# A one-layer language-model tower on one core: idle-time products on TensorE, weight pieces and rank reads regrouped

## The chip, the core and the metric

The kernel runs on one core of a Trainium2 chip. The metric is the time of one execution on the device in microseconds (us), the median of several runs. The five engines of the core are TensorE (PE; its weight loads are shown apart as PEld), VectorE (DVE), ScalarE (ACT), GpSimd (POOL) and SyncE (SP), which only issues transfers here. Engines run their own instruction lists in order and wait for each other through semaphores.

## The reference, cut to what matters

```python
h = tok(x)                                  # softmax of 4 coefficients per token times 4 base rows, + bias; 4096 tokens x 256
p = layernorm(h) @ Wv.T + bv                # q = k = v = p, 16 heads of 16, batches of 1024 tokens
attn = softmax(p_h @ p_h.T / 4) @ p_h       # per head, 4 batches
h = h + attn @ Wo.T + bo
logits = layernorm(h) @ router              # 8 experts, the 2 best of each token, softmax of the two
hidden = silu(xn @ w13_gate) * (xn @ w13_up)   # 512 wide, per expert
h = h + sum over the two experts of weight * (hidden @ w2)
```

## The kernel before

Everything runs in one launch. `attention` comes first, then `experts`. Attention works in 16 groups (`GROUPS`), four per batch of 1024 tokens (`HG` is 4); a group is four heads. Of each group there are 64 score tiles of 128x512 (items). Three items make a unit: PE computes them (`scores`, L347), ACT takes their exponential in one 128x1536 instruction (L758), and PE sums four of them at a time against the values (`sums`, L359). PE's program is written out by hand: behind each such quad the function `after` may place other products, by the quad's number in its group: `fold` and `turn` of the group before, `tile_rows`, the two halves of the next group's query features (`query_product`, L334), and `rank`.

In some groups PE prepares the next batch: `preparing(grp, 1)` is true in groups 1, 5 and 9 (tokens are turned, L479), `preparing(grp, 2)` in groups 2, 6 and 10 (keys are turned, L485); in group 12 `worst_own` (L530) stands at the same place. Each of these three waits for `u_read` of the second half, that is for DVE's instruction L788 of that half.

DVE has one list per group: the normalisation of the group before last, `fold_out`, `places_out`, `copy_rows`, then `query_features` half 0 (L786, L788, L790, L794), `choose` (the two best experts, L829 to L837), `query_features` half 1, `weigh` (L898 to L900), `rank_read_out` (L905 to L907), and at the end the copy of the accumulated sums out of PSUM (L1245), on which `fold` waits. In the last group (`LAST`, 15) it also does, before that copy, what is left of group 14: `rank_read_out`, `places_out` (to L923), `normalise` (L842 to L859) and `normal_rows` (L868 to L871).

POOL works beside this on the expert weights. Each of 24 pieces (512 KB) is loaded by SP (L256), and split into a bf16 high part (a cast, L700) and a bf16 low part (a subtraction of two SBUF operands, L631). `pieces_of` deals the first 19 (`BESIDE`) out to the groups, one each and two in groups 5, 10 and 15. Between them POOL writes the slots of the tokens (`note`, L637). Of the last five pieces ACT makes the high part once the exponentials are over (L732), POOL the low one; a load may start once the low part three pieces back is done.

The tail of attention is a chain between DVE and PE: copy of the sums (L1245), `fold` (L379), `turn` (L386), `last_rows` (L414), `choose`, `rank` (L435), the tile counts and places on DVE, `slot_table` (L419, L421), and the indices (L962) by which POOL gathers the rows of the first four expert tiles. SP turns them by DMA; PE's first expert product (L1472) and DVE's L1549 wait for the first of them. PE meanwhile does a last product on `near_p` (L624) and twelve products without use (L626), and then walks the expert tiles.

Set-up does the same for the constants and the first batch: `weights_and_keys`, `turn_tokens`, `turn_keys`, `own_scores`, then the two query products of group 0.

## Time and profile before

| | us |
|---|---|
| median of 3 runs | 871.98 |
| lowest and highest | 871.75, 874.14 |
| the profiled execution | 876.0 |
| its span, first to last instruction | 874.2 |
| PE busy in the span | 767.1 |
| ACT busy | 544.6 |
| DVE busy | 510.9 |
| POOL busy | 355.0 |

The profiled execution took 876.0 us, of which 1.8 us lie outside the span. Times in the rows below are counted from the start of the span. Attention with its tail ends at about 579 us, the experts take the rest. A row of the timeline gives the start, the duration, the engine, the line of the kernel, the operation and its operands, how many instructions were merged, and in brackets how long the engine had been idle before and what ended that.

### The profile page before, as it was taken

What the parts mean: (1) busy time and instruction counts of PE and PEld (TensorE: products, weight loads), DVE (VectorE), ACT (ScalarE), POOL (GpSimd) and SP (SyncE); (2) the same over time, 40 slices, a digit from 0 to 9 for tenths busy, and PEclk for the clock granted to TensorE, in tenths of its full rate; (3) what the DMA queues carried; (4) which work ended last, traced back from release to release, by engine and by line L of the source; (5) the groups of instructions that cost most, each with busy time, mean ns of one, the idle gap of its engine ahead of it and who ended that gap; (6) DMA issues with size and microseconds to landing.
All of it is one profiled execution on the core that took longest, in us unless ns stands there. A gap on an engine that the chain in (4) does not pass through costs nothing.

```text
span 874.2 us, 16623 instructions
## 1 busy us (share of the span) xinstructions
PE 767.1 (88%) x5249; PEld 300.0 (34%) x5250; DVE 510.9 (58%) x1623; ACT 544.6 (62%) x515; POOL 355.0 (41%) x305
## 2 busy tenths in 40 slices
PE   3699994999999999989999997289999999999992
PEld 1233220222222222222222221135555555555551
DVE  7644563576667558676756478654555555545540
ACT  0468993999989999989999997312222222222221
POOL 6760030302411330241133217256666666666652
PEclk9589996899999999999999999579999999999997
DMA  2030105012011101201110124349999999999973
GB/s 40 2 94 1 37 12 38 13 37 74 13 37 49 46 16 37 74 14 37 49 50 14 37 73 98 87 85 166 159 162 164 158 162 163 160 163 156 154 122 44
DMA packets 141362, 67.72 MB, mean 77 GB/s; under 512 B 114822, under 2 KB 136984, under 8 KB 141294
## 3 DMA queue, kind: packets, MB, share of 16 engines
q1 hardware_dynamic: 125262, 49.33, 27.5%
q0 software_dynamic: 16032, 17.55, 13.9%
q8 instruction: 35, 0.57, 0.4%
q14 instruction: 33, 0.27, 0.2%
HBM read 22.52 MB, written 17.57 MB: 46 GB/s over the span
## 4 chain that ended last, share of the span: by engine, by line
PE 69%; DVE 16%; ACT 5%; issue 5%; DMA 2%; another core or an unknown queue 1%; POOL 0%; SPq 0%; POOLq 0%; ACTq 0%; DVEq 0%
PE PS L359 20%; PE PS L1472 18%; PE PS L1481 10%; PE PS L347 9%; ACT shared L758 5%; PE PS L402 2%; PE PS L379 2%; DVE room L788 2%; DVE room L794 2%; PE PS L403 2%; DVE room L786 2%; PE PS L445 1%; DMA room<-room 1%; DVE room L790 1%
## 5 line engine op out<-in xcount | busy, mean ns | idle before, releaser
L758 ACT ACTIVATE shared<-PS 128x1536 f32<-128x1536 f32 x342 | 464.8, 1519 | 48.5 <-PE PS L347 36.3
L359 PE MATMUL PS<-shared,va 128*32 128x512 f32 x2048 | 279.8, 619 | 5.1 <-DVE room L1245 4.7
L637 POOL DMA_INDIRECT slots<-pair_no,room x60 | 59.5, 991 | 364.3 <-DVE room L917 350.6
L1472 PE MATMUL PS<-w_p,room 128*128 x816 | 186.7, 379 | 0.0
L347 PE MATMUL PS<-room,ak 32*128 32x512 bf16 x1024 | 137.5, 394 | 14.3 <-ACT shared L758 9.5
L1522 ACT ACTIVATE shared<-PS 128x512 f32<-128x512 f32 x68 | 40.6, 598 | 162.9 <-PE PS L1472 162.9
L1438 POOL DMA_INDIRECT out<-room,idx_tok x68 | 110.9, 1631 | 67.1 <-ACT room L1527 38.6
L1553 DVE SCALAR_TENSOR_TENSOR shared<-shared,room,PS 128x512 f32<-128x512 f32 x68 | 50.8, 748 | 124.5 <-ACT shared L1522 124.5
L1481 PE MATMUL PS<-shared,room 128*128 x816 | 101.1, 273 | 8.6 <-issue 5.9
L1472 PEld LDWEIGHTS PS<-w_p,room 128*128 128x128 f16 x816 | 79.8, 98 | 82.9 <-issue 0.6
L347 PEld LDWEIGHTS PS<-room,ak 32*128 32x128 bf16 x1024 | 33.5, 91 | 215.6 <-ACT shared L758 166.8
L1421 POOL DMA_INDIRECT room<-xrows,idx_tok x68 | 71.8, 1056 | 48.6 <-issue 28.2
L1481 PEld LDWEIGHTS PS<-shared,room 128*128 128x128 bf16 x816 | 76.2, 97 | 40.8 <-issue 27.0
L359 PEld LDWEIGHTS PS<-shared,va 128*32 128x32 f32 x2048 | 40.7, 109 | 67.2 <-issue 56.0
L1527 ACT COPY room<-PS 128x256 f32<-128x256 f32 x68 | 25.3, 372 | 61.5 <-PE PS L1481 60.8
L823 DVE COPY room<-PS 128x264 f32<-128x264 f32 x32 | 13.8, 433 | 65.8 <-PE PS L403 64.0
L1560 DVE TENSOR_TENSOR room<-shared,room 128x512 bf16<-128x512 f32 x67 | 46.4, 692 | 2.3
L1558 DVE CAST room<-shared 128x512 bf16<-128x512 f32 x67 | 35.0, 522 | 2.3
L644 POOL DMA_INDIRECT cw<-coeff,xi x32 | 31.1, 971 | 10.8 <-issue 9.3
L631 POOL TENSOR_TENSOR w_p<-room,w_p 128x1024 bf16<-128x1024 f32 x16 | 34.4, 2147 | 1.4
L786 DVE CAST room<-PS 128x512 bf16<-128x512 f32 x32 | 22.0, 688 | 18.5 <-PE PS L334 18.5
L794 DVE SCALAR_TENSOR_TENSOR room<-room,part_c 128x512 bf16<-128x512 bf16 x32 | 27.6, 861 | 1.1
(283 smaller groups left out, 616.2 us busy)
## 6 DMA issues: line engine op xcount, KB each, us to landing
room<-w SPq DMA_DIRECT2D x24, 512.0 KB, 4.9
xrows<-room SPq DMA_DIRECT2D x16, 258.0 KB, 3.2
out<-room SPq DMA_DIRECT2D x16, 256.0 KB
room<-room SPq DMA_TRANSPOSE x135, 4.1
room<-xrows,idx_tok POOLq DMA_INDIRECT x68
out<-room,idx_tok POOLq DMA_INDIRECT x68
slots<-pair_no,room POOLq DMA_INDIRECT x60
xT<-xT SPq DMA_DIRECT2D x3, 256.0 KB, 4.3
```

The costliest lines, as they stand in the source:

```text
L347: last = pe.matmul(PS[:, WIDE * (u % BUFS) + i, :], g.ak[r, k0:k0 + P], qf[r, grp % 2, 512 * c:512 * c + 512], start=True, stop=True)
L359: last = pe.matmul(PS[32 * slot:32 * slot + 32, ACC, :], g.va[:, KT * (grp // HG) + kt, c, :], prob[:, (4 * quad + slot) % (RING * WIDE), ...
L637: pool.indirect_dma_start(g.slots, bass.IndirectOffsetOnAxis(pos_i[:, grp % 2, 2 * k + kk:2 * k + kk + 1].bitcast(U32), 0), g.pair_no[:, t ...
L758: act.activation(prob[:, at:at + n, :].rearrange("p n q -> p (n q)"), PS[:, buf:buf + n, :].rearrange("p c q -> p (c q)"), ACT.Exp).then_i ...
L794: dve.scalar_tensor_tensor(qf[:, grp % 2, 512 * half:512 * half + 512], u2[:], g.part_c[:, 1:2], ures[:], ALU.mult, ALU.add).then_inc(qf_r ...
L1421: pool.indirect_dma_start(xs_w[:, j % XBUF, :], None, g.xrows, bass.IndirectOffsetOnAxis(g.idx_tok[:, j:j + 1].bitcast(U32), 0), bounds_ch ...
L1438: pool.indirect_dma_start(out, bass.IndirectOffsetOnAxis(g.idx_tok[:, m:m + 1].bitcast(U32), 0), y_s[:, m % XBUF, :], None, bounds_check=T ...
L1472: last = pe.matmul(PS[:, up_bank(k) + half, :], xsT[:, k, 2 * a + c, :], g.w13_p[:, w, c, ds(e, 1), FF * half:FF * half + FF].rearrange("p ...
L1481: last = pe.matmul(PS[:, YB[k % 2], 0:D], hidT[:, k, 4 * a + c, :], g.w2_p[:, w, c, ds(e, 1), :].rearrange("p e d -> p (e d)"), start=n == ...
L1522: act.activation(act_s[:], PS[:, up_bank(k), :], ACT.Silu).then_inc(silu_done, 1)
L1553: dve.scalar_tensor_tensor(hid[:], act_s[:], weight[:, k % 2:k % 2 + 1], PS[:, up_bank(k) + 1, :], ALU.mult, ALU.mult).then_inc(hid_ready, 1)
L1560: dve.tensor_tensor(halves[:, k, 1], hid[:], halves[:, k, 0], ALU.subtract).then_inc(hid_split, 1)
```

## The change

There are four edits. `warm(bank, count)` issues products of which nothing is used: 64 rows (partitions 64 to 127 of `xq`) by 128 columns, against 512 columns, in bf16. In set-up 12 stand behind `weights_and_keys`, 5 behind `own_scores`, 4 and 2 behind the two query products and 6 behind the first scores. In the tail 2, 4 and 6 stand behind `fold`, `turn` and `last_rows`, 11 behind a new wait for the places of the last group, and 8 behind `slot_table`; the twelve products at the end become eighteen. `pieces_of` deals the pieces 14 to 18 out as two, two, one and none to groups 12 to 15. In the groups that prepare a batch (`crowded`) `choose` comes behind the second half of the query features. In the last group `normalise` and `normal_rows` come ahead of `rank_read_out` and `places_out`.

```diff
     def pieces_of(grp):
-        return range(BESIDE * grp // GROUPS, BESIDE * (grp + 1) // GROUPS)
+        if grp < GROUPS - HG:
+            return range(BESIDE * grp // GROUPS, BESIDE * (grp + 1) // GROUPS)
+        done = BESIDE * (GROUPS - HG) // GROUPS
+        return range(min(done + 2 * (grp - GROUPS + HG), BESIDE), min(done + 2 * (grp - GROUPS + HG) + 2, BESIDE))
...
+        def warm(bank, count):
+            for _ in range(count):
+                pe.matmul(PS[:, bank, :], g.xq[XR0:P, 0:P], g.xq[XR0:P, 0:512], start=True, stop=True)
...
             weights_and_keys()
+            pe.wait_ge(xq_set, 1)
+            warm(UB, 12)
             turn_tokens(0, 0, 0)
             turn_tokens(0, 1, 1)
             turn_keys(0, 2)
             pe.wait_ge(kq_in, 16 * NA)
             pe.wait_ge(kr_copied, 1)
             own_scores(0, 4)
+            warm(UB, 5)
         query_product(0, 0)
+        if initial:
+            warm(ACC, 4)
         query_product(0, 1)
+        if initial:
+            warm(ACC, 2)
         for u in range(BUFS - 1):
             scores(u)
+        if initial:
+            warm(ACC, 6)
...
         fold(LAST)
+        warm(4, 2)
         turn(LAST)
+        warm(4, 4)
         last_rows()
+        warm(4, 6)
         rank(LAST)
+        pe.wait_ge(pos_ready, GROUPS)
+        warm(4, 11)
         slot_table()
+        warm(4, 8)
         pe.wait_ge(near_ready, 1)
         pe.matmul(PS[0:1, 5, 0:1], near_p[:], g.ones[:, 0:1], start=True, stop=True).then_inc(near_mm, 1)
-        for n in range(12):
+        for n in range(18):
             pe.matmul(PS[:, 0, :], g.ones_b[:], g.ak[:, 0:512], start=True, stop=True)
...
-            if grp >= 1:
+            crowded = preparing(grp, 1) or preparing(grp, 2)
+            if grp >= 1 and not crowded:
                 choose(grp - 1)
             if grp + 1 < GROUPS:
                 query_features(grp + 1, 1)
+            if grp >= 1 and crowded:
+                choose(grp - 1)
...
             if grp == LAST:
+                normalise(grp - 1)
+                normal_rows(grp - 1)
                 rank_read_out(grp - 1)
                 places_out(grp - 1)
-                normalise(grp - 1)
-                normal_rows(grp - 1)
```

The change adds 26 lines in all, so a line of the changed kernel has a number up to 26 higher. First, POOL in the last four groups, from piece 15 on: `note` is the row with DMA, a piece the pair of a CAST and a TENSOR_TENSOR. Before:

```order
L700 CAST w_p<-room 128x1024
L631 TENSOR_TENSOR w_p<-room,w_p 128x1024
L637 DMA slots<-pair_no,room 49152x1 x4
L700 CAST shared<-room 128x1024
L631 TENSOR_TENSOR shared<-room,shared 128x1024
L637 DMA slots<-pair_no,room 49152x1 x4
L700 CAST shared<-room 128x1024
L631 TENSOR_TENSOR shared<-room,shared 128x1024
L700 CAST shared<-room 128x1024
L631 TENSOR_TENSOR shared<-room,shared 128x1024
L637 DMA slots<-pair_no,room 49152x1 x4
L631 TENSOR_TENSOR shared<-room,shared 128x1024 x3
```

The same pieces in the changed kernel, where piece 15 is the second of group 12:

```order
L723 CAST w_p<-room 128x1024
L654 TENSOR_TENSOR w_p<-room,w_p 128x1024
L660 DMA slots<-pair_no,room 49152x1 x4
L723 CAST shared<-room 128x1024
L654 TENSOR_TENSOR shared<-room,shared 128x1024
L723 CAST shared<-room 128x1024
L654 TENSOR_TENSOR shared<-room,shared 128x1024
L660 DMA slots<-pair_no,room 49152x1 x4
L723 CAST shared<-room 128x1024
L654 TENSOR_TENSOR shared<-room,shared 128x1024
L660 DMA slots<-pair_no,room 49152x1 x8
L654 TENSOR_TENSOR shared<-room,shared 128x1024 x3
```

The pair of pieces moved from the last group to group 13 (a second one went to group 12), and two notes now follow each other with nothing between.

Second, DVE in the last group, from the end of `choose` on. Before:

```order
L837 TENSOR_TENSOR room<-room 128x16
L898 TENSOR_SCALAR room<-room 128x2
L899 RECIPROCAL room<-room 128x2
L900 SCALAR_TENSOR_TENSOR room<-room 128x2
L905 TENSOR_TENSOR room<-room,PS 128x8
L906 TENSOR_TENSOR room<-room,PS 128x8
L907 TENSOR_TENSOR room<-PS,room 128x16
L912 TENSOR_TENSOR room<-room 128x32
L914 TENSOR_REDUCE room<-room 128x4
L917 CAST room<-room 128x4
```

And in the changed kernel:

```order
L860 TENSOR_TENSOR room<-room 128x16
L921 TENSOR_SCALAR room<-room 128x2
L922 RECIPROCAL room<-room 128x2
L923 SCALAR_TENSOR_TENSOR room<-room 128x2
L865 BN_STATS room<-room 128x6 x2
L867 TENSOR_TENSOR room<-room 128x2
L868 TENSOR_TENSOR room<-room 128x2
L869 TENSOR_TENSOR room<-room 128x2
L870 TENSOR_TENSOR room<-room 128x2
L871 TENSOR_SCALAR room<-room 128x2
```

The statistics of the normalisation (BN_STATS) stand directly behind `weigh`; the reads of the ranks follow after the normal rows.

Third, PE in the tail, from `turn` to the last products without use. Before:

```order
L386 MATMUL PS<-ident,room 64x128 x2
L414 MATMUL PS<-pair,room 128x264 x2
L435 MATMUL PS<-room,tri_b 128x16
L436 MATMUL PS<-room,ones_b 128x16
L419 MATMUL PS<-room 128x74 x4
L421 MATMUL PS<-ident,room 128x74
L624 MATMUL PS<-ones,room 1x1
L626 MATMUL PS<-ak,ones_b 128x512 x12
```

And in the changed kernel:

```order
L390 MATMUL PS<-ident,room 64x128 x2
L534 MATMUL PS<-xq 128x512 x4
L418 MATMUL PS<-pair,room 128x264 x2
L534 MATMUL PS<-xq 128x512 x6
L439 MATMUL PS<-room,tri_b 128x16
L440 MATMUL PS<-room,ones_b 128x16
L534 MATMUL PS<-xq 128x512 x11
L423 MATMUL PS<-room 128x74 x4
L425 MATMUL PS<-ident,room 128x74
L534 MATMUL PS<-xq 128x512 x8
L647 MATMUL PS<-ones,room 1x1
L649 MATMUL PS<-ak,ones_b 128x512 x18
```

The products of line 534 stand between the products of the chain, each group behind the one whose result DVE works on next.

## Rows read from the trace of the kernel before

**Rows 1.** Page, parts 2 and 5: granted clock by slice of 21.9 us; a group of instructions.

```profile
PEclk9589996899999999999999999579999999999997
...
L758 ACT ACTIVATE shared<-PS 128x1536 f32<-128x1536 f32 x342 | 464.8, 1519 | 48.5 <-PE PS L347 36.3
```

**Rows 2.** Timeline of PE and ACT, set-up and first exponentials.

```profile
22.02 1.94 PE L479 MATMUL PS<-ident,w_p 128*98 128x128 f32 x8 [5.63 <-DVE w_p L1005]
...
29.01 0.61 PE L334 MATMUL PS<-xq,krb 128*128 128x512 bf16 x1 [2.22 <-DVE krb L1044]
...
35.20 1.03 PE L347 MATMUL PS<-room,ak 32*128 32x512 bf16 x5 [2.15 <-DVE room L794]
...
35.84 4.13 ACT L758 ACTIVATE shared<-PS 128x1536 f32<-128x1536 f32 x3 [1.30 <-PE PS L347]
...
52.78 1.45 ACT L758 ACTIVATE shared<-PS 128x1536 f32<-128x1536 f32 x1 [1.82 <-PE PS L347]
```

**Rows 3.** Windows: busy us of PE, PEld, DVE, ACT, POOL; granted clock; DMA share, GB/s.

```profile
152.00:156.00 4.00, 4.00 (x19) 0.43 (x17) 2.97 (x11) 2.61 (x2) 0.00 (x0) 0.50 0.00 0
...
575.00:579.00 4.00, 4.00 (x11) 1.36 (x9) 0.00 (x0) 0.00 (x0) 3.37 (x4) 0.50 0.62 108
```

**Rows 4.** Timeline of groups 5, 6, 9, 10 and 12: DVE, PE and ACT.

```profile
235.56 2.51 DVE L794 SCALAR_TENSOR_TENSOR room<-room,part_c 128x512 bf16<-128x512 bf16 x1
239.30 0.68 DVE L786 CAST room<-PS 128x512 bf16<-128x512 f32 x1
240.82 0.91 PE L479 MATMUL PS<-ident,w_p 128*98 128x128 f32 x4 [2.49 <-DVE room L788]
242.32 1.45 ACT L758 ACTIVATE shared<-PS 128x1536 f32<-128x1536 f32 x1 [2.74 <-PE PS L347]
...
271.50 9.71 ACT L758 ACTIVATE shared<-PS 128x1536 f32<-128x1536 f32 x7 [0.48 <-PE PS L347]
...
361.39 10.85 ACT L758 ACTIVATE shared<-PS 128x1536 f32<-128x1536 f32 x8 [0.69 <-PE PS L347]
...
392.71 5.48 ACT L758 ACTIVATE shared<-PS 128x1536 f32<-128x1536 f32 x4 [1.67 <-PE PS L347]
...
450.54 0.17 PE L530 MATMUL PS<-ident,room 16*1 16x16 f32 x1 [0.73 <-DVE room L788]
```

**Rows 5.** Timeline of the last group: POOL, DVE and PE.

```profile
530.14 2.13 POOL L631 TENSOR_TENSOR shared<-room,shared 128x1024 bf16<-128x1024 f32 x1
530.15 2.16 DVE L837 TENSOR_TENSOR room<-room 128x16 bf16<-128x16 f32 x1
...
533.52 1.98 DVE L900 SCALAR_TENSOR_TENSOR room<-room 128x2 f32<-128x2 f32 x1
...
537.22 0.75 DVE L842 BATCH_NORM_STATS2 room<-room 128x6 f32<-128x256 f32 x2
...
540.28 1.07 PE L359 MATMUL PS<-shared,va 128*32 128x512 f32 x8 [0.45 <-ACT shared L758]
...
543.17 2.58 DVE L871 TENSOR_TENSOR room<-room 128x512 f16<-128x512 f32 x1
545.67 0.68 DVE L1245 TENSOR_SCALAR room<-PS 128x512 f32<-128x512 f32 x1
```

**Rows 6.** Timeline of the tail: PE and DVE.

```profile
546.41 1.97 PE L379 MATMUL PS<-fold_sel,room 128*128 128x64 f32 x8 [3.97 <-DVE room L1245]
...
554.85 0.17 DVE L837 TENSOR_TENSOR room<-room 128x16 bf16<-128x16 f32 x1
...
568.93 1.99 PE L419 MATMUL PS<-room 128*128 128x74 f32 x8 [13.63 <-DVE room L886]
...
574.08 0.19 PE L624 MATMUL PS<-ones,room 128*1 128x1 f32 x2 [2.73 <-DVE room L972]
574.20 5.11 PE L626 MATMUL PS<-ak,ones_b 128*128 128x512 bf16 x12
...
579.20 0.27 DVE L1549 TENSOR_SCALAR room<-second,room 128x1 f32 x1 [4.40 <-DMA room<-room]
```

## What the change does to the time: the prediction

> **What bounds the kernel now.** I read the page's first parts, then the timeline by stage. Between 35 and 541 us ACT sets the pace: 342 exponentials make 464.8 us, with only 48.5 us idle between them [rows 1]. In that stage an edit is worth what it takes from ACT's idle time. Before it (set-up) and behind it (tail) there is one chain from DVE to PE and back, and an edit is worth what it takes from that chain. From 579 us on PE walks the expert tiles, which the change leaves alone. The reader is to see three losses. First, the clock line reads 5 in the second slice: PE was granted 1.2 GHz instead of 2.4 through the second slice and a part of the third, some 25 us [rows 1], and seven exponentials from 35.84 to 52.78 took 16.9 us where three in a row take 4.13 [rows 2]. Second, ACT idles in the groups that prepare a batch, 2.74 us at worst, since PE stands at a product that waits for DVE's L788 [rows 4]. Third, in the last group DVE is late: the last sums are done at 541.3, but DVE copies them at 545.67 [rows 5], and `fold` starts only at 546.41 [rows 6].
>
> **Products in set-up: +0.4 us.** One such product takes 0.427 us at 1.2 GHz (twelve in 5.11 [rows 6]), half of that at 2.4. At the low rate 12 take 5.1, 5 take 2.1, 4 take 1.7, 2 take 0.9 and 6 take 2.6 us. The twelve and the five lie in idle time of 5.63 and 2.22 us [rows 2]. The four and the two (2.6 us) lie between the first query product, which ends at 29.6, and the first scores, which end 2.15 us ahead of 35.20 and last 0.6: 2.8 us, of which the second query product needs 0.4. That just fits. The six have 2.15 us [rows 2] and stick out by 0.4 ahead of the second exponential: +0.4. What they could bring is the clock. If it stands at 2.4 GHz from about 31 us on, the seven exponentials go at 1.38 us each, 9.7 in place of 16.9, less some 0.8 for DVE's answers in between: -6.5.
>
> Does it rise? It rose at the end of a stretch in which twelve products of 128 rows ran (574.2 to 579.3) [rows 3, 6]. It did not from 152 to 156, though PE was never idle there; what ran were the sums with 128 rows and products of 32 and 34 rows [rows 3]. The new ones have 64 rows, between the two, and I find them nearer to the second: half of the array is unused. I forecast no rise.
>
> The page "TensorE: Matmul & The Clock Gate" of the Trainium skill says under "What's actually happening" that the default is throttled "and activity releases the throttle", and speaks of no rows. By that rule the clock rises in set-up; no row of this trace shows 64-row products.
>
> **`choose` behind the second half, in groups 1, 2, 5, 6, 9, 10: -4.6 us.** In group 5 DVE ends the first half at 238.07 and begins the second at 239.30 [rows 4]: `choose` lies between, 1.2 us. Moved, it lets L788 end 1.2 us earlier in groups 5 and 10, where the first half ends late; in groups 6 and 9 only about 0.7, because the product it reads comes later. ACT's waits are 2.74, 0.48, 0.69 and 1.67 us in groups 5, 6, 9 and 10 [rows 4]. Gains: 1.2, 0.5, 0.65 and 1.2; in group 5 another 0.9, an estimate: PE idles 1.3 instead of 2.5 us, so the clock may stay up for the two products of about 1 us behind it; 0.2 in group 2, none in group 1, where PE does not wait. What is late next is `rank`, which waits for `choose`; it stands several products behind, and I find it short by 0.4 us in groups 2 and 5, which is already taken off.
>
> **Pieces two, two, one, none: +1.7 us in group 12.** The reason of group 5's loss is a second piece. L794, normally 0.75 us, took 2.51 because POOL's subtraction of two SBUF operands ran [rows 4]; likewise L837 took 2.16 beside an L631 of 2.13 [rows 5]. Groups 12 and 13 now have two pieces, and `choose` is not moved there. In group 12 PE's L530 waits for the same L788, 0.73 us so far and without idle time on ACT [rows 4]. With 1.8 us more it waits 2.5. In group 10 a PE wait of nearly 2 us left ACT 1.67 idle, so I take 1.7; the bounds are 0 and group 5's 2.74 with the 0.9 behind it, 3.7. In group 13 no product waits for that half before `rank`; I take 0, up to 2.
>
> The page "SBUF — State Buffer" of the Trainium skill, section "Who interferes with whom", calls this pair of ports an exclusive lock, in which the later instruction waits for the whole of the earlier. The trace agrees, 2.16 beside 2.13 us, and the rule speaks against this edit in group 12.
>
> **Last group and front of the tail: -3.9 us.** Without pieces DVE's L837 takes its usual 0.17 us [rows 6] instead of 2.16, and its neighbours lose their blocks too. `weigh`, which ended with L900 at 535.50 [rows 5], is over by about 530 (L837 began before 530.15; three short instructions are left). Normalisation and normal rows took from 537.22 to the end of L871 at 545.75, 8.5 us, of which some 1.9 are L871's block, since POOL's next subtraction ran [rows 5]; without it 6.6, so they end at about 536.6. The ranks and places, which took from 535.50 to 537.22 [rows 5], follow to 538.3. So DVE waits at 541.4 for the last sums instead of the reverse: L1245 moves from 545.67 to 541.4: -4.25 [rows 5]. This is the surest term. `fold` then follows PE's own work closely and runs at 2.4 GHz, half of 1.97 us [rows 6]: -0.9. `turn` and the last rows I leave at the low clock. There the four fillers (1.7 us) end 0.5 us behind DVE's blocks and the six (2.6 us) 0.75 us behind the choice: +1.25. Sum -3.9 at the start of `rank`. SP's load of piece 19 no longer waits behind the late `weigh`; this is hidden, it only lets ACT's casts follow each other.
>
> **Rest of the tail: +1.9 us.** The eleven stand in PE's idle stretch of 13.63 us [rows 6], but begin only when the places are out. They take 4.7 us; behind the places DVE still has some twenty instructions ahead of `slot_table`, by my estimate 5 us, so I take 0; the bounds are 0 and 1. The eight take 3.4 us in a gap of 2.73 [rows 6]: +0.7 before the product on `near_p`. The twelve ended together with the arrival of the first turned rows, on which DVE's L1549 waited until 579.20 [rows 6], so neither was late. Eighteen of 128 rows, begun at the low clock, take 7.7 us if it never rises; as in the rows of before it rises after some 4.8 us: eleven slow, seven quick, 6.2 us. PE is then ready at 574.1 - 3.9 + 0.7 + 6.2 = 577.1, and the rows arrive at 579.2 - 3.9 = 575.3. The first expert product starts at 577.2 and not at 579.2: tail and last group together -2.0.
>
> **Sum.** +0.4 - 4.6 + 1.7 - 2.0 = -4.5: the profiled 876.0 becomes 871.5. The median of the runs is 4.0 us below that execution; I carry the difference over unchanged: 871.98 - 4.5 = 867.5.
>
> **Rivals.** (a) The 64-row products lift the clock. Set-up then gives -6.5 and not +0.4. In the tail all fillers run at half the time and none sticks out; `turn` and the last rows save 1.2 us more, less 0.6 because `choose` now meets POOL's last subtraction; the first expert product follows the arrival of its rows: -5.4 in place of -2.0. Sum -6.5 - 4.6 + 1.7 - 5.4 = -14.8: 857.2. For it speaks that no product of 64 rows is in these rows, so that nothing excludes it; against it the continuous stretch without a rise [rows 3]. This is also the rival that goes by the Trainium skill's rule named above, which no row here shows for such products.
>
> (b) The second piece costs more: group 12 like group 5 (3.7) and group 13 up to 2. Then -4.5 + 2.0 + 2.0 = -0.5: 871.5, no difference to be seen.
>
> (c) Slower: the fillers hold up work that is ready. All of them stay at the low clock: 0.4 in set-up, 1.25 ahead of `rank`, 0.7 ahead of `near_p`, and 18 instead of 12 give 7.7 - 5.1 = 2.6, in sum 4.95. It decides once the two gains on DVE come to less than about 2.3 us; if they come to nothing, 876.9. Against it: the gap of 4.3 us ahead of L1245 stands plainly in the timeline [rows 5].
>
> **How the numbers follow.** A measurement of this kernel tells 0.3% (2.6 us) from no change. Chances: the forecast 0.52, (a) 0.27, (b) 0.14, (c) 0.07. Of the forecast's 0.52, a tenth lies above 869.4. Faster: 0.47 + 0.27 = 0.74; same: 0.05 + 0.14 = 0.19; slower 0.07. The range reaches down to (a) with about 1.5 us for its phase, and up to (b): 855.5 to 871.5. It leaves out (c) and the edges. The forecast's own range is 864.5 to 870.5: group 12 between 0 and 3.7, and the eighteen between 3.9 and 7.7 us.
>
> **What would show it.** Forecast: granted clock still low from 23 to about 45 us and again from about 545 us; the second exponential 0.4 us later; ACT without idle time over 1.6 us in groups 5, 6, 9 and 10; a wait of PE's `worst_own` near 2.5 us with L794 near 2.5 us in group 12; no block of DVE between 528 and 541; L1245 right behind the last sums; the first expert product waiting for the fillers. Wrong: a clock of 2.4 GHz at 31 us makes it (a); ACT idle in groups 12 and 13 by more than 3 us makes it (b); DVE's L1245 still 4 us behind the last sums takes the largest term away.

## The result: 0.6% slower, where 0.5% faster was forecast

| | us |
|---|---|
| changed kernel, median of 9 runs | 878.43 (875.12 to 882.35) |
| kernel before, median of 9 runs beside them | 873.54 (871.75 to 876.62) |
| ratio, 95% interval | 1.0059 (1.0037 to 1.0082) |
| profiled execution of the changed kernel, and its span | 875.12, 873.4 |
| span of before | 874.2 |

The change costs some 5 us; the forecast was a gain of 4.5. All ratios of this document, here and for the kernels of the experiments, are taken over the executions within 1.5% of the quickest of their kernel (for `shift29` five of twelve, for `late_loads` four of six), while the medians are of all executions, and the one trace that fell outside, of `pieces_only`, is not used. The profiled execution is the quickest of the nine, so its trace shows where each step came out, but not yet the whole loss: that took traces of more executions (below). First its clock line and its exponentials, from the page, beside [rows 1]:

```profile
PEclk9589996999999999999999998789999999999997
...
L781 ACT ACTIVATE shared<-PS 128x1536 f32<-128x1536 f32 x342 | 465.3, 1519 | 50.1 <-PE PS L351 39.4
```

ACT's idle time did not shrink (50.1 us, 48.5 before): the stage that ACT paces gained nothing. The stages, by the start of DVE's copy of the sums (L1245 before, L1271 now), in this first pair of traces:

```
                                        before     after    gained (-) or lost (+)
copy of group 0 starts                   79.93     80.54    +0.6  set-up
group 2, and 3 (a standstill in 2)       75.3      72.9     -2.4
group 5 / 6 / 9 / 10 (`choose` moved)    32.87 30.02 29.36 31.44 -> 32.16 30.58 28.88 31.27   -0.8 in sum
group 12 (second piece)                  29.00     32.10    +3.1
group 15 (no piece, ranks later)         32.71     31.85    -0.9
copy of group 15 to the end of the span 328.5     328.1     -0.4
```

The gain of 2.4 us in groups 2 and 3 lies at the standstill near 140 us, which ended sooner (ACT waited 9.65 us, 11.15 before), and behind it, where the clock came back sooner. `choose` is moved in group 2 too, but a gain of that size isn't shown to be its work: the two groups take 70.8 to 76.9 us in the twelve traces in which it is moved and 72.3 to 79.4 in the seven others. Without these two groups this execution is 1.6 us behind.

**Set-up.** Timeline of PE, then windows (columns as in [rows 3]):

```profile
26.62 2.31 PE L534 MATMUL PS<-xq 64*128 64x512 bf16 x5
...
33.31 2.74 PE L534 MATMUL PS<-xq 64*128 64x512 bf16 x6
```

```profile
28.00:32.00 4.00, 4.00 (x10) 0.78 (x9) 3.33 (x9) 0.00 (x0) 2.88 (x4) 0.50 0.05 2
32.00:36.00 4.00, 4.00 (x15) 0.84 (x15) 3.82 (x7) 1.45 (x1) 3.14 (x3) 0.50 0.08 2
```

PE is busy without a gap and the granted clock stays at 0.50, that is 1.2 GHz. As forecast, no rise comes in this trace, and the first exponentials come a little later.

**Group 5**, where `choose` is moved, PE, DVE and ACT, answering [rows 4]:

```profile
237.81 0.65 PE L483 MATMUL PS<-ident,w_p 128*98 128x128 f32 x4 [1.30 <-DVE room L811]
238.82 1.45 ACT L781 ACTIVATE shared<-PS 128x1536 f32<-128x1536 f32 x1 [1.06 <-PE PS L351]
...
240.15 0.17 DVE L860 TENSOR_TENSOR room<-room 128x16 bf16<-128x16 f32 x1
...
240.83 0.69 DVE L1048 COPY xT<-PS 34x512 f32<-34x512 f32 x1
...
241.67 0.17 PE L439 MATMUL PS<-room,tri_b 128*128 128x16 bf16 x1 [1.90 <-DVE xT L1048]
...
242.23 1.45 ACT L781 ACTIVATE shared<-PS 128x1536 f32<-128x1536 f32 x1 [1.96 <-PE PS L351]
```

The first wait shrank by 1.2 us as forecast (2.49 to 1.30). But a second one stands behind it: `rank` (L439) waits 1.90 us, and not for `choose`, whose last instruction was over at 240.32, but for the copy of the turned tokens (L1048, ended 241.52). In the code `rank` of these groups waits for `xT_copied` or `xq_copied`. That copy stands on DVE behind both the second half and `choose`; whichever of the two comes first, it ends at the same time. So ACT's waits there, 2.74 and 0.99 us before, are 1.06 and 1.96 now, and hardly shorter in sum. In group 6, where ACT had waited only 0.48, it is 0.29 and 0.83 now, and the group is 0.6 us longer. Even the gain of 0.7 us in group 5 does not stand against a second trace of the kernel before: in `before_again` that group takes 32.16 us as well. Over all traces, groups 5, 6, 9 and 10 take 123.9 us in sum with `choose` moved (mean of twelve) and 124.0 without (mean of seven).

**Group 12**, with its second piece:

```profile
444.07 2.30 POOL L654 TENSOR_TENSOR w_p<-room,w_p 128x1024 bf16<-128x1024 f32 x1
...
444.41 2.51 DVE L817 SCALAR_TENSOR_TENSOR room<-room,part_c 128x512 bf16<-128x512 bf16 x1
...
449.68 0.18 PE L538 MATMUL PS<-ident,room 16*1 16x16 f32 x1 [2.50 <-DVE room L811]
...
450.22 1.94 PE L363 MATMUL PS<-shared,va 128*32 128x512 f32 x8
450.34 1.45 ACT L781 ACTIVATE shared<-PS 128x1536 f32<-128x1536 f32 x1 [1.92 <-PE PS L351]
...
452.75 8.36 ACT L781 ACTIVATE shared<-PS 128x1536 f32<-128x1536 f32 x6 [0.96 <-PE PS L351]
```

This is the chain that was forecast: DVE's L817 held 2.51 us beside POOL's subtraction, a wait of 2.50 at `worst_own` (2.5 forecast), 1.92 us of idle time on ACT (1.7 forecast). The 0.96 behind it the forecast had only in its upper bound: PE had been idle for 2.5 us, its clock fell, and the next sums took 1.94 us instead of 1.06.

**Last group and tail**, DVE and PE, answering [rows 5, 6]:

```profile
536.63 0.39 PE L351 MATMUL PS<-room,ak 32*128 32x512 bf16 x3 [1.27 <-issue]
...
541.49 3.64 PE L363 MATMUL PS<-shared,va 128*32 128x512 f32 x16
...
545.27 0.69 DVE L1271 TENSOR_SCALAR room<-PS 128x512 f32<-128x512 f32 x1 [7.25 <-PE PS L363]
...
548.33 1.03 PE L534 MATMUL PS<-xq 64*128 64x512 bf16 x4
...
572.97 5.54 PE L649 MATMUL PS<-ak,ones_b 128*128 128x512 bf16 x18
```

The waiting was turned round, as forecast: DVE waits 7.25 us for the sums, where the sums had waited 4.3 us for DVE. But the sums come at 545.2 instead of 541.4: PE stood for 1.27 us with no reason that the trace knows and then fell to the low clock. The clock rose again at the copy, before the first product without use (547.08), so four of them took 1.03 us. This is luck: of the eight traces with the 64-row products in the tail only `again2` has it too. In these two the clock then stayed up for 10 us, beside the first twelve of them; in `reorders` and `no_tail`, which have none there, such a stretch is 7 us long. So the products may help to hold a clock that is up; no run tests it.

### The profile page after: what moved, and what is told of

Read it like the earlier page. It is cut to its first block, busy times and chain, and to the rows that moved or that the text cites. A ratio compares the mean times of both kernels' runs of the same rounds, so it can differ in the third digit from the quotient of the medians.

```text
span 873.4 us, 16756 instructions
## 1 busy us (share of the span) xinstructions
PE 788.8 (90%) x5315; PEld 304.7 (35%) x5316; DVE 507.0 (58%) x1623; ACT 544.9 (62%) x515; POOL 355.2 (41%) x305
## 4 chain that ended last, share of the span: by engine, by line
PE 73%; DVE 13%; ACT 5%; issue 5%; DMA 1%; another core or an unknown queue 1%; POOL 1%; DVEq 0%; ACTq 0%; POOLq 0%; SPq 0%
PE PS L363 21%; PE PS L1498 19%; PE PS L1507 10%; PE PS L351 9%; ACT shared L781 5%; PE PS L406 2%; DVE room L817 2%; PE PS L383 2%; PE PS L407 2%; DVE room L811 1%; PE PS L534 1%; DVE room L809 1%; PE PS L449 1%; PE PS L338 1%
## 5 line engine op out<-in xcount | busy, mean ns | idle before, releaser
L781 ACT ACTIVATE shared<-PS 128x1536 f32<-128x1536 f32 x342 | 465.3, 1519 | 50.1 <-PE PS L351 39.4
L654 POOL TENSOR_TENSOR w_p<-room,w_p 128x1024 bf16<-128x1024 f32 x16 | 34.7, 2166 | 1.4
L817 DVE SCALAR_TENSOR_TENSOR room<-room,part_c 128x512 bf16<-128x512 bf16 x32 | 31.1, 971 | 1.1
```

The lines of the kernel that those rows point to most:

```text
L781: act.activation(prob[:, at:at + n, :].rearrange("p n q -> p (n q)"), PS[:, buf:buf + n, :].rearrange("p c q -> p (c q)"), ACT.Exp).then_i ...
L817: dve.scalar_tensor_tensor(qf[:, grp % 2, 512 * half:512 * half + 512], u2[:], g.part_c[:, 1:2], ures[:], ALU.mult, ALU.add).then_inc(qf_r ...
```

## The experiments

Each kernel was timed beside the kernel before on its chip; a row gives the medians and the ratio with its interval. The level differs from chip to chip: before takes 872 to 876 us on some and 885 to 890 on others, so only ratios are compared.

| kernel | its median, before's median | ratio (95%) |
|---|---|---|
| again (changed kernel) | 890.77, 888.90 | 1.0028 (1.0003 to 1.0053) |
| no_setup | 896.20, 888.90 | 1.0082 (1.0054 to 1.0110) |
| no_tail | 888.78, 888.90 | 0.9993 (0.9966 to 1.0021) |
| old_pieces | 886.49, 888.90 | 0.9970 (0.9947 to 0.9993) |
| before_again | 886.65, 886.43 | 0.9999 (0.9962 to 1.0035) |
| pieces_only | 888.76, 886.43 | 1.0015 (0.9983 to 1.0048) |
| late_loads | 898.62, 886.43 | 1.0116 (1.0055 to 1.0177) |
| reorders | 884.79, 886.43 | 0.9986 (0.9955 to 1.0017) |
| tail_only | 892.17, 890.26 | 1.0017 (0.9996 to 1.0039) |
| setup_only | 884.67, 890.26 | 0.9945 (0.9919 to 0.9972) |
| shift29 | 888.19, 890.26 | 0.9845 (0.9807 to 0.9882) |
| tail128 | 890.10, 890.26 | 1.0001 (0.9981 to 1.0020) |
| again2 (changed kernel) | 894.96, 885.08 | 1.0119 (1.0066 to 1.0173) |
| setup_again | 885.65, 885.08 | 1.0013 (0.9981 to 1.0045) |
| setup_and_orders | 884.35, 885.08 | 0.9980 (0.9948 to 1.0013) |
| mend12 | 890.21, 885.08 | 1.0042 (1.0007 to 1.0077) |
| setup128 | 874.08, 875.52 | 0.9976 (0.9956 to 0.9995) |
| best128 | 873.19, 875.52 | 0.9981 (0.9958 to 1.0005) |

And what the traces give of all but `pieces_only`, one execution each, in us (length of a group from copy to copy; the last column runs from the last copy to the end of the span; group 12 and the last group in the kernels with the new pieces are marked *):

```
                  group 12   group 15   rest
before              29.00      32.71    328.5
before_again        29.53      32.92    329.1
tail_only           29.76      33.94    330.6
setup_only          29.76      34.54    329.8
shift29             29.74      36.82    326.1
setup_again         29.52      35.42    332.7
setup128            29.00      30.81    330.0
reorders            29.58      33.44    328.2
setup_and_orders    29.51      30.82    331.7
old_pieces          29.74      30.90    334.3
best128             29.00      30.52    329.8
after               32.10*     31.85*   328.1
again               32.43*     35.74*   333.9
again2              32.31*     39.84*   327.8
no_setup            31.25*     35.29*   333.1
no_tail             31.14*     32.12*   329.1
late_loads          32.34*     34.36*   337.5
tail128             32.37*     35.61*   328.4
mend12              30.26*     32.76*   334.4
```

### The change with one part undone

`again` is the changed kernel. `no_setup` and `no_tail` leave out products of which nothing is used:

```diff
# no_setup
-            pe.wait_ge(xq_set, 1)
-            warm(UB, 12)
...
-            warm(UB, 5)
...
-            warm(ACC, 4)
...
-            warm(ACC, 2)
...
-            warm(ACC, 6)
# no_tail
-        warm(4, 2)
...
-        warm(4, 4)
...
-        warm(4, 6)
...
-        pe.wait_ge(pos_ready, GROUPS)
-        warm(4, 11)
...
-        warm(4, 8)
...
-        for n in range(18):
+        for n in range(12):
# old_pieces: pieces_of as before
```

> The changed kernel once more, on the chip of the next three. Measured so far: 0.59% (about 5 us) above before, while its profiled execution has nearly before's span; that execution shows 0.6 us more in set-up, 3.1 lost in group 12 and last sums that end at 545.2 instead of 541.3. All theories expect 3 to 7 us above before here. The theory of a chance disturbance expects a profile in which the group ends stand elsewhere than in the first one; the theory of a steady cost expects group 12 and the last group to lose the same again.

> The changed kernel without the 29 products in set-up, all else as changed. Theory S (the products in set-up hold up work and nothing else): 0.6 us below the changed kernel. Theory T (the products of the tail and what they do to code loading cost the time): no more than 0.6 below. If it falls by 2 us or more, the products in set-up shift something later, and the profile shows where.

> The changed kernel without the 31 products between the last sums and the choice's read-out, and with 12 products ahead of the experts as before. Theory T (they cost the time): 3 us or more below the changed kernel, since PE no longer has unrolled products to fetch and to run ahead of work that is ready. Theory L (the last group loses because the loads come sooner and PE waits for its code beside them): within 1 us of the changed kernel, last sums again near 545. In the profiled execution the front of the tail was 1.9 us quicker than before with them, so by that reading alone it gets 1 to 2 us slower.

> The changed kernel with the pieces spread as before (one each in groups 11 to 14, two in the last). Theory P (the second piece in group 12 costs 3.1 us, and the loads brought forward cost PE 3.4 us in the last group): 3 to 6 us below the changed kernel, group 12 without idle time on ACT, last sums back at the pace of ACT. The forecast's reason (pieces of the last group hold up DVE) expects DVE late again in the last group, and together less than 2 us below the changed kernel. Theory T: no change beyond 1 us.

The pieces came out most plainly: on one chip the changed kernel stands at 1.0028 and without the new spread at 0.9970, 5 us less. In the traces 2.7 us of it lie in group 12. Without the products of the tail the ratio is lower by 3 us (1.0028 against 0.9993; by the medians 2 us), as theory T had it, but the two intervals overlap. The tail of `again`, timeline of ACT and PE:

```profile
548.82 1.45 ACT L781 ACTIVATE shared<-PS 128x1536 f32<-128x1536 f32 x1 [2.33 <-remote]
...
553.11 0.60 ACT L781 ACTIVATE shared<-PS 128x512 f32<-128x512 f32 x1 [2.84 <-remote]
...
560.82 1.88 PE L534 MATMUL PS<-xq 64*128 64x512 bf16 x4
...
564.69 2.74 PE L534 MATMUL PS<-xq 64*128 64x512 bf16 x6
567.36 0.20 PE L439 MATMUL PS<-room,tri_b 128*128 128x16 bf16 x1
...
593.06 7.07 PE L1498 MATMUL PS<-w_p,room 128*128 x32
```

```profile
588.00:592.00 4.00, 4.00 (x13) 1.46 (x12) 0.00 (x0) 0.00 (x0) 3.68 (x3) 0.59 0.79 145
592.00:596.00 4.00, 4.00 (x20) 1.84 (x19) 0.27 (x1) 0.15 (x1) 2.19 (x2) 1.00 0.41 70
```

Here the tail runs at 1.2 GHz up to the last products without use (the second fence has two windows, columns as in [rows 3]). DVE's choice is made at 566.55, and the rank product starts at 567.36, right behind the six products, which held it up by 0.8 us; the four ahead of `last_rows` had cost 0.5 before. The rank product stands 11.5 us behind the copy of the sums (10.3 in `before_again`, which is at the low clock too), the first expert product 37.2 us (34.4). The experts take 296.7 us instead of 294.7, but not for the clock, which is at 1.00 when they begin; in `tail_only`, with the same products in the tail, they take 293.9. What these 2 us are stays open. `no_setup` contradicts its expectation: slower by 0.54% with less work. Its trace has a standstill more in group 3 (2.7 us, no known releaser), which no edit touches. So more than the parts' own costs moves this kernel's time.

### One part alone, and the loads

```diff
# pieces_only: before with the new pieces_of.  reorders: before with both orders on DVE.
# late_loads: the changed kernel, and in SP's program
+        sp.wait_ge(summed, GQUADS * GROUPS)
         for n in range(BESIDE, len(pieces)):
             load(n)
```

> The kernel before, unchanged, for a trace on the same chip as the other three. Its time against itself is 1.000 within 0.3%. In group 12 it takes 29.0 us between the copies of the sums (29.00 in the first trace) and in the last group 32.7 us, if those two numbers are steady; a theory of chance in code loading expects them to differ by 2 us or more.

> The kernel before with one edit: pieces two, two, one, none in the last four groups. Theory P+L: group 12 takes 3 us more than before; in the last group ACT has to wait 2 to 5 us for its own code, which stands behind three loads of 512 KB that SP now issues 5 us sooner; DVE is still early enough or late by 0 to 2 us less than before. In sum 3 to 7 us slower than before. The forecast's reason: 1.7 lost, 2 to 4 gained, so 0 to 2 us quicker.

> The changed kernel with SP waiting for the last sums before it issues the loads of the tail. Theory L (those loads delay the code of ACT and PE in the last group): no idle time of ACT of over 1 us in the last group, which then takes 31 us and not 35 to 36, so 3 to 5 us below the changed kernel, that is 0 to 2 us below before. Rival (PE or ACT lose this time whatever the loads do, since the unrolled products move the code): last group 35 us again, no change.

> The kernel before with the two orders on DVE alone: the choice behind the second half in the crowded groups, and the normalisation ahead of the ranks in the last. No products added, pieces as before. All theories expect it quicker than before: 0.7 us from group 5 (measured), about nothing from groups 6, 9 and 10 in sum, 2 us from the last group (30.9 us with the old pieces in place of 32.7). So 2 to 3 us below before, 0.3%.

Theory L, by which the loads make ACT wait in the last group, falls. With the loads held back ACT still waited there, and the kernel became slower: ACT's cast then waited 9.26 us for its piece. From `late_loads`, ACT:

```profile
554.34 0.60 ACT L782 ACTIVATE shared<-PS 128x512 f32<-128x512 f32 x1 [4.24 <-remote]
...
564.29 1.04 ACT L756 CAST shared<-room 128x1024 bf16<-128x1024 f32 x1 [9.26 <-DMA room<-w]
```

`before_again` shows such waits as well (2.12 and 1.53 us), where the first trace of before had none. So they come without the change too. By the medians the two orders alone bring 1.6 us and the spread of pieces alone costs 2.3; both intervals include no difference at all.

### Products: in set-up, in the tail, and on how many rows

```diff
# shift29: before, ahead of turn_tokens(0, 0, 0)
+            pe.wait_ge(xq_set, 1)
+            for _ in range(29):
+                pe.matmul(PS[:, UB, 0:1], g.xq[XR0:P, 0:P], g.xq[XR0:P, 0:1], start=True, stop=True)
# tail128: the changed kernel with, in the tail's five places,
+        def warm_all(count):
+            for _ in range(count):
+                pe.matmul(PS[:, 4, :], g.ones_b[:], g.ak[:, 0:512], start=True, stop=True)
```

> The kernel before with only the products of the tail (31, and 18 instead of 12). Theory T (they run at 1.2 GHz and hold up work that is ready): 2 us more ahead of the rank product, 1 to 2 more up to the first expert product, which comes 37 us and not 34.4 after the last group's copy; and 1.5 us more in the expert stage, which then begins at the low clock. In sum 4 to 5 us slower than before. Rival, by the forecast: the rank product 1.25 later and the rest hidden, 1 to 3 us slower.

> The kernel before with only the 29 products in set-up. Theory S (they hold up the first exponentials and do not lift the clock): the first exponential 0.4 to 1.2 us later, 0.5 to 1 us slower in all. Rival, place of code: the time differs from before by 2 us or more in either way, and the trace shows it behind 55 us, where nothing was changed, as stalls with no releaser that the trace knows.

> The kernel before with 29 products of a single column at one place of set-up where PE idles: as many instructions more as the products of set-up add, but no work. Theory S: no change (within 0.3%). Rival, place of code: the same difference to before as the kernel with only the set-up products shows, 2 us or more in either way.

> The changed kernel with the products of the tail on all 128 rows instead of 64, as many and as long. If the clock rises by how much of the array works, it stands at 2.4 GHz when the ranks are made and again in the expert stage's first microseconds: the tail takes 5 us less than with 64 rows, 0.5% below the changed kernel. If rows do not matter, its clock stays at 0.5 from the fold on and its time is the changed kernel's.

`tail_only` and `tail128` ran on one chip, with as many products in the same places, equally wide, on 64 and on 128 rows. `tail128` has the rest of the change as well, but `again`, which differs from it in these products alone, had a granted clock of 0.50 from 556 to 588 us. Windows of the two (columns as in [rows 3]), first `tail_only`:

```profile
564.00:568.00 4.00, 4.00 (x11) 1.46 (x10) 1.55 (x7) 0.22 (x1) 3.49 (x2) 0.50 0.64 164
568.00:572.00 4.00, 3.90 (x11) 1.17 (x9) 2.49 (x15) 0.00 (x0) 0.00 (x0) 0.50 0.28 98
...
584.00:588.00 4.00, 3.91 (x15) 2.53 (x14) 3.53 (x13) 1.03 (x2) 0.00 (x0) 0.50 0.14 47
588.00:592.00 4.00, 3.67 (x11) 1.24 (x11) 2.69 (x13) 0.00 (x0) 2.06 (x3) 0.50 0.12 33
```

and `tail128`:

```profile
564.00:568.00 4.00, 4.00 (x12) 2.20 (x12) 1.73 (x7) 0.00 (x0) 3.21 (x2) 0.54 0.78 214
568.00:572.00 4.00, 1.59 (x9) 0.53 (x7) 3.40 (x24) 0.00 (x0) 0.00 (x0) 1.00 0.33 114
...
584.00:588.00 4.00, 3.30 (x18) 2.10 (x18) 3.73 (x13) 0.00 (x0) 0.83 (x1) 0.90 0.00 0
588.00:592.00 4.00, 3.39 (x17) 1.67 (x19) 0.79 (x5) 0.00 (x0) 3.09 (x4) 1.00 0.40 91
```

PE is equally busy up to 568, and only with 128 rows is the clock at 1.00, that is 2.4 GHz, right behind. The first expert product then stands 33.6 us behind the copy of the sums, not 36.7. But rows aren't the only difference. The 64-row products read partitions 64 to 127 of `xq`, which the kernel fills with 1.0 and never writes again, so both their operands are constant; those on 128 rows read ones against the keys here, and the identity matrix in the kernels further below. No kernel ran varying data on 64 rows or constant data on 128. That the number of rows decides is therefore not shown, only that these products leave the clock low and those lift it. `tail_only` is 1.9 us slower than before by the medians, at the edge of its interval.

`setup_only` was 0.55% faster, against theory S; the traces put this into groups 2 and 3 (72.3 us, 76.3 in `before_again`, which ran on another chip), 100 us behind the products. `shift29` warns of what such a number is worth. It adds 29 products of a single column, of which nothing is used, and its twelve executions lie in two clumps, 873 to 877 and 883 to 892 us. So its ratio of 0.9845 is not to be read as a gain of the kernel: the median of all twelve is 0.23% below before. I can't say what chooses the clump.

### Which of these repeat, and group 12 mended

```diff
# setup_again: as setup_only.  setup_and_orders: before with the set-up products and both orders.  mend12:
-            crowded = preparing(grp, 1) or preparing(grp, 2)
+            crowded = preparing(grp, 1) or preparing(grp, 2) or grp == GROUPS - HG
```

> The changed kernel on a third set of runs. If its parts are steady costs (3 us in group 12, 3 to 5 us in tail and first experts, against some 3 us less at the standstill near 150 us): 0.3 to 0.6% slower than before. If the losses were chance of the chip: within 0.3% of before.

> The kernel before with only the 29 products in set-up, once more. If the gain of 0.55% is steady: 0.3 to 0.6% faster again, with groups 2 and 3 together near 72 us, where before has 76. If chance: within 0.3%, groups 2 and 3 together at 75 us or more, set-up 0.6 us longer.

> The parts that alone were not slower: products in set-up, the choice behind the second half, the normalisation ahead of the ranks; pieces as before, no products in the tail. If the parts add up: 0.5 to 0.7% faster than before. If the set-up gain was chance: within 0.3%.

> The changed kernel with the choice behind the second half in group 12 too. Forecast's mechanism (DVE, held up by POOL's subtraction, gives the rows on which the product of the worst own score and the next ones wait): the choice's 1.2 us leave that path, PE waits 1.3 instead of 2.5 us and keeps its clock, group 12 takes 30 to 30.7 us instead of 32.1 to 32.4: 1.5 to 2.4 us, 0.2 to 0.3% below the changed kernel. Rival (the extra time of group 12 is something else): group 12 stays over 31.5 us.

The loss of the changed kernel repeats, in three sets of runs: 1.0059, 1.0028, 1.0119. The gain of the set-up products does not: 0.9945, then 1.0013. `mend12` confirms how group 12 loses most of its time; PE's row there:

```profile
459.44 0.17 PE L538 MATMUL PS<-ident,room 16*1 16x16 f32 x1 [1.02 <-DVE room L811]
```

The wait falls from 2.50 to 1.02 and the group from 32 to 30.26 us. Here the reordering works, because `rank` waits for `flag_set`, which is set soon: it waits 0.52 us. `again2` had the longest last group of all, 39.84 us; its ACT rows:

```profile
553.41 1.45 ACT L781 ACTIVATE shared<-PS 128x1536 f32<-128x1536 f32 x1 [4.67 <-remote]
557.77 2.79 ACT L781 ACTIVATE shared<-PS 128x1536 f32<-128x1536 f32 x2 [2.91 <-remote]
```

### The change with its two faults mended

```diff
# in warm, for setup128 (set-up only, all else as before) and best128 (the whole change, pieces as before)
-                pe.matmul(PS[:, bank, :], g.xq[XR0:P, 0:P], g.xq[XR0:P, 0:512], start=True, stop=True)
+                pe.matmul(PS[:, bank, :].rearrange("p (a b) -> p a b", a=4), g.identb[:],
+                          g.identb[:].unsqueeze(1).to_broadcast([P, 4, P]), start=True, stop=True)
```

> The kernel before with only the 29 products in set-up, on all 128 rows (the identity against itself, same width and number). If rows decide, as in the tail: the clock stands at 2.4 GHz within the stretch from 28 to 45 us, the exponentials of the first quads follow each other in under 2 us, and the first group ends up to 6 us sooner; in time 2 to 6 us, 0.2 to 0.7%, faster than before, less what the standstill near 50 us covers. If not: clock 0.5 up to 50 us, within 0.3% of before.

> The whole change with two mends: all its products on 128 rows, and the pieces spread as before. If the costs found are the right ones (group 12 about 2.6 us, the tail 3 us at the low clock) and the clock rises: 0.5 to 1% faster than before. If the costs are right and the clock of set-up does not rise: 0.2 to 0.5% faster. If it is not faster at all, something else than these two made the changed kernel slower.

With these products on 128 rows the clock of set-up does rise. Windows of `setup128`, to be held beside those of the changed kernel above, and its exponentials:

```profile
28.00:32.00 4.00, 3.35 (x11) 0.84 (x9) 3.33 (x9) 0.00 (x0) 3.04 (x4) 0.79 0.06 2
32.00:36.00 4.00, 2.78 (x16) 0.80 (x15) 3.82 (x7) 1.77 (x2) 3.13 (x3) 1.00 0.07 2
```

```profile
35.68 5.48 ACT L772 ACTIVATE shared<-PS 128x1536 f32<-128x1536 f32 x4 [1.29 <-PE PS L347]
```

Between 36 and 130 us the clock then stays at 1.00, in `best128` too. The 64-row products are in set-up in eleven traces. In seven of them the clock is low up to 50 us and longer; in four (`setup_again`, `setup_and_orders`, `again2`, `late_loads`) it rises for some 3.4 us near 30 us and falls again, while the products still run. From `setup_again`:

```profile
30.00:33.00 3.00, 1.79 (x10) 0.47 (x6) 2.82 (x8) 1.29 (x2) 2.39 (x3) 1.00 0.08 2
34.00:36.00 2.00, 2.00 (x5) 0.38 (x4) 1.90 (x4) 0.00 (x0) 1.70 (x2) 0.50 0.09 2
```

`no_setup`, which has no such products, shows the same short rise (0.95 between 30 and 33 us), so it isn't shown to be their work.

The copy of group 0 starts at 76.71 and not at 79.93, 3.2 us sooner, and the kernel is 0.24% faster (0.05 to 0.44%). `best128` has the same gain in set-up, 29.00 us in group 12 and the shortest last group (30.52 us), and yet its interval ends at 1.0005. What it gains in the last group it gives back in the tail, timeline of DVE and POOL:

```profile
549.33 2.43 DVE L854 CAST room<-room 128x4 f32<-128x4 uint32 x1
...
545.43 6.29 POOL L651 TENSOR_TENSOR shared<-room,shared 128x1024 bf16<-128x1024 f32 x3
```

`choose` meets POOL's three subtractions: 2.43 us for an instruction that takes 0.17. They start 4.9 us behind the copy of the sums here; in the changed kernel, where POOL has no piece in the last group, they start 1.0 us behind it (546.3) and are over before `choose`. `old_pieces` (2.70), `setup_and_orders` (2.83), `reorders` (1.97) and `setup128` (2.04) show the same block; `before_again`, whose subtractions start 1.2 us behind the copy, does not.

## Why the prediction was wrong

- **Set-up, +0.4 us and no rise of the clock: right.** +0.6 in the first pair of traces, clock at 0.50 throughout. (Before the change the low stretch was 31 us long, from 19 to 50 us, not "some 25".) No trace has a rise that is shown to be the work of 64-row products. The rule on activity of the Trainium skill's page "TensorE: Matmul & The Clock Gate", section "What's actually happening", by which they release the throttle, did not hold for them in seven of eleven traces. The reason given, that half of the array is unused, stays unproven: the products that did lift the clock had more rows and other data.
- **`choose` behind the second half, -4.6 us: this step failed.** It brought 0.8 us in the first pair and 0.1 on average over all traces. "What is late next is `rank`, which waits for `choose`" named the wrong wait. The copy of the turned tokens or keys was next, and it stands behind both orders. It was in the code and in the list on DVE, and I followed only the wait that I had meant to shorten.
- **Group 12, +1.7 us: right mechanism, too small.** It measured 3.1 us in the first pair, 2.5 us as the mean of seven traces against eleven (31.99 and 29.47). The wait was as forecast; the fall of the clock behind it was put into the upper bound of 3.7 and not into the sum, though group 5 had shown it.
- **Last group, -4.25 us, "the surest term": this failed too.** DVE does get ready in time, 7.25 us before the sums. But the gap of 4.3 us could be won only as far as nothing else holds up the last sums, and ACT's waits with no known releaser do: 0 us in the first trace of before, 3.65 in `before_again`, whose last sums end at 555.9 and whose copy starts at 555.94. The gap was not one execution's alone. `setup128` keeps the old orders and pieces, its ACT doesn't stand, and there the copy comes 2.5 us behind the last sums:

```profile
537.60 1.07 PE L359 MATMUL PS<-shared,va 128*32 128x512 f32 x8 [0.45 <-ACT shared L772]
...
541.11 0.68 DVE L1259 TENSOR_SCALAR room<-PS 128x512 f32<-128x512 f32 x1
```

  The last group took 34.7 us on average in the eight traces with the new pieces (31.85 to 39.84), 33.9 in the seven with old pieces and old orders (30.8 to 36.8), and 31.4 in the four with old pieces and new orders (30.5 to 33.4). ACT's waits in it, 0 to 7.6 us, go with its length. So the new orders may have gained here and the new pieces lost it again; why ACT stands less in those four isn't shown. Where its waits are short and the pieces are as before, `choose` in the tail meets POOL and gives 2 us back, where the forecast had put 0.6 and only in rival (a). The 0.9 us of a quick `fold` came in two of the changed kernel's three traces, those with the clock up at the copy.
- **Products of the tail, +1.25 ahead of `rank` and +1.9 behind it: right.** In `again` against `before_again` the rank product comes 1.2 us later; the eleven cost nothing, the eight 0.7 and the eighteen 1.0, so the first expert product comes 2.8 us later, where the forecast's two terms make 3.15. These costs were to be hidden behind the gains of the last group, which did not come.
- **The rivals.** The measured loss, 4.9 us, is close to rival (c)'s 4.95, but this is partly chance. Its mechanism is there: fillers at the low clock hold up work that is ready. But they cost 0.6 in set-up and 2.8 in the tail, 3.4 and not 4.95 (it put 2.6 on the eighteen), while the 2.5 of group 12 and the 0.8 by which the last group is longer on average are not in its sum. It was given 7 in 100. Its condition was that the gains on DVE come to nothing, and they nearly did. Rival (a), the lifted clock, did not come about: no trace has a lasting rise beside the 64-row products in set-up.

What stays open: what the standstills are. DVE and ACT stand together for 7 to 11 us between 135 and 158 us in every trace; DVE stands 8.6 to 9.5 us near 50 us in the traces at the level of 885 us, of before as of the others, and not in those at 872, so this one makes most of the difference in level; ACT stands in the last group. Two rows of DVE from `before_again` stand below. Their lengths depend on more than the edit, so single parts of this change can't be added up to the whole: tail alone +0.17%, set-up alone -0.55% or +0.13%, orders alone -0.14%, pieces alone +0.15%, all together +0.3 to +1.2%. It wasn't tried to move the code of ACT. One lead lies in the traces: in `before`, with all four engines idle from 140 to 145 us, the transfer engines are busy all that time (share 1.04) and move only 31 GB/s, while near 50 us in `before_again` they are nearly idle (0.05 from 42 to 50 us). So the standstills needn't have one cause.

```profile
50.51 0.17 DVE L1151 SCALAR_TENSOR_TENSOR room<-PS,rt_s 128x16 f32<-128x16 f32 x1 [8.62 <-remote]
...
154.30 0.69 DVE L1030 COPY ak<-PS 128x1024 bf16<-128x1024 bf16 x1 [10.46 <-remote]
```

The end of a wait is put down to a releaser that the trace does not know; both instructions read products that PE had finished long before, at 45.7 (L453) and 142.7 us (L485).

## What to carry to other kernels

Before an instruction is moved out of one wait's way, list every wait of the consumer that is late next, and look where those producers stand in the list: what stands behind both places gains nothing. Products without use pay only if they lift the clock. Here those on 128 rows, with the identity matrix or the keys as data, did, and those on 64 rows of ones did not; at the low clock each is a delay for whatever is ready behind it. A gap that one profiled execution shows ahead of the critical step is worth only what no other wait covers in the next execution; a second trace of the kernel before would have shown that here.

## What the runs showed of the hardware

- With 64-row products of constant ones among its own work PE was busy for all of 28 to 36 us in set-up with the granted clock at 0.50 (changed kernel); with as many products on 128 rows it was at 0.79 and then 1.00 (`setup128`), and in the tail at 0.54 and then 1.00 (`tail128`). The data of the two kinds differ too, and no run separates data from rows.
- With 29 one-column products more, the executions of a kernel lay between 873 and 892 us, where before lay between 886 and 895 on that chip.
- A cast of 128x4 elements on DVE took 2.43 us, not 0.17, beside POOL's subtraction of SBUF operands.
